# Turning norm factors straight from their column: four layers of attention and experts on one core

## The reference, cut to what matters

```python
xn = _layernorm(x)                      # (x - mean) / sqrt(var + 1e-5), over the 128 features
x = x + _L0_attn_ref(xn, ...) + _L0_ffn_ref(xn, ...)   # window attention; small mixer + 8 experts, top 2
xn = _layernorm(x)
x = x + _L1_attn_ref(xn, ...) + _L1_ffn_ref(xn, ...)   # differential attention; 8 experts, top 2
xn = _layernorm(x)
x = x + _L2_attn_ref(xn, ...) + _L2_ffn_ref(xn, ...)   # full attention; gated low-rank layer
xn = _layernorm(x)
x = x + _L3_attn_ref(xn, ...) + _L3_ffn_ref(xn, ...)   # flow attention; dequantized feed-forward
```

```python
q = rmsnorm((x @ wq.T).reshape(B, T, 16, 64), q_norm_w)
k = rmsnorm((x @ wk.T).reshape(B, T, 4, 64), k_norm_w)
```

## Time and profile before

| what | value |
|---|---|
| runs, us | 1449.86, 1451.62, 1457.27; median 1451.62 |
| profiled execution, us | 1449.79, its span 1448.0 |
| PE busy | 1291.5 us (89%) |
| DVE, ACT, POOL busy | 913.3, 664.0, 302.3 us |
| mean granted TensorE clock | 0.926 of full |

### The profile page before, as it was taken

One profiled execution on the slowest core, in us unless ns is written; L12 is line 12 of the kernel. 1 busy time (PEld: TensorE's weight loads), 2 busy tenths in 40 slices (PEclk: granted clock), 3 DMA queues, 4 the chain that ended last, 5 costly groups with the idle time before them and its releaser, 6 DMA issues.

```text
span 1448.0 us, 23894 instructions
## 1 busy us (share of the span) xinstructions
PE 1291.5 (89%) x9334; PEld 791.3 (55%) x9334; DVE 913.3 (63%) x1975; ACT 664.0 (46%) x1424; POOL 302.3 (21%) x309
## 2 busy tenths in 40 slices
PE   6878697997997888779899979999799989899998
PEld 4456565876674666445666757755344323224555
DVE  4478753343354568865687657677578868775366
ACT  2345042762651322016443535566466646576621
POOL 1242072000102510474001201044421312101000
PEclk8988698998998879759999989999999989999999
DMA  8000023332100220123523463321330121200000
GB/s 247 21 1 1 1 85 120 89 106 70 29 8 18 57 39 4 62 66 71 144 85 99 123 163 105 121 69 30 66 74 4 33 39 34 36 1 29 1 8 22
DMA packets 65101, 86.23 MB, mean 60 GB/s; under 512 B 9566, under 2 KB 49374, under 8 KB 63326
## 3 DMA queue, kind: packets, MB, share of 16 engines
q1 hardware_dynamic: 60892, 76.30, 20.1%
q0 software_dynamic: 4096, 8.40, 2.0%
HBM read 62.19 MB, written 22.48 MB: 58 GB/s over the span
## 4 chain that ended last, share of the span: by engine, by line
PE 63%; DVE 13%; DMA 9%; POOL 5%; issue 4%; ACT 3%; SPq 3%; DVEq 0%; ACTq 0%; POOLq 0%
PE psB L420 29%; PE psA L420 27%; PE psB L424 5%; DMA wA<-slots_x 3%; DVE mx L1478 2%; POOL slots_x L1945 2%; DMA arena<-scr1k 2%; PE psA L424 2%; DMA arena<-scr2k 2%; DVE st L1177 1%; ACT pbuf L1807 1%; ACT pbuf L1725 1%; DMA arena<-slots_x 1%; SPq L2049 1%; DMA scr1k<-arena 1%
## 5 line engine op out<-in xcount | busy, mean ns | idle before, releaser
L1807 ACT ACTIVATE pbuf<-psA 128x512 f32<-128x512 f32 (+3 forms) x768 | 350.6, 489 | 249.0 <-PE psA L420 241.1
L1478 DVE TENSOR_REDUCE mx<-psA 128x1 f32<-128x512 f32 (+3 forms) x520 | 326.0, 660 | 83.5 <-PE psA L420 80.7
L420 PE MATMUL psA<-arena 64*64 64x128 f32 (+6 forms) x1504 | 187.9, 291 | 2.2 <-ACT pbuf L1807 1.4
L420 PEld LDWEIGHTS psA<-arena 64*64 64x64 f32 (+3 forms) x1504 | 111.1, 135 | 70.4 <-ACT pbuf L1807 30.6
L1725 ACT ACTIVATE pbuf<-psA,st,rq 128x128 f32<-128x128 f32 x256 | 92.7, 467 | 99.9 <-DVE st L1181 99.9
L420 PE MATMUL psA<-arena,w 96*128 96x512 bf16 (+4 forms) x320 | 112.7, 404 | 6.1 <-DMA arena<-scr2k 3.3
L420 PE MATMUL psA<-w_mdiagT,w_identb 128*128 128x128 bf16 x512 | 108.8, 222 | 0.0
L420 PE MATMUL psB<-pbuf,arena 128*5 128x512 f32 (+3 forms) x1024 | 93.4, 438 | 0.5 <-ACT pbuf L1807 0.4
L420 PE MATMUL psB<-xf,wA 128*128 128x128 f32 x624 | 93.0, 294 | 0.0
L1904 POOL TENSOR_TENSOR sm<-sm,w_ohalf 128x4 f32<-128x4 f32 x24 | 24.5, 1030 | 294.7 <-DVE sm L1048 294.7
L420 PEld LDWEIGHTS psB<-xf,wA 128*128 128x128 f32 x624 | 81.5, 203 | 7.6 <-issue 2.4
(11 more groups left out here) (318 smaller groups left out, 2325.5 us busy)
## 6 DMA issues: line engine op xcount, KB each, us to landing
wA<-in_moe SPq DMA_DIRECT2D x39, 576.0 KB, 3.8
wA<-in_moe SPq DMA_DIRECT2D x39, 256.0 KB, 3.1
slots_x<-wA SPq DMA_DIRECT2D x20, 256.0 KB, 3.7
slots_y<-tH SPq DMA_DIRECT2D x18, 256.0 KB, 3.7
wA<-slots_x SPq DMA_DIRECT2D x15, 256.0 KB, 4.0
arena<-scr2k SPq DMA_DIRECT2D x48, 64.0 KB
scr1q<-arena SPq DMA_DIRECT2D x4, 384.0 KB, 3.9
scr1k<-arena SPq DMA_DIRECT2D x4, 384.0 KB, 4.2
```

The costliest lines, as they stand in the source:

```text
L420: return pe.matmul(out, lhsT, rhs, start=start, stop=stop, skip_group_check=True)
L1478: dv.tensor_reduce(m[:, t, h:h + c], maxb(lay, b, n)("mx", lay, b, n)[:, 0:c * k].rearrange("p (c k) -> p c k", c=c), AX.X, ALU.max) \
L1807: ac.activation(pb(lay, b, s, j)[:, 0:T - q0_], scoreb("ex", lay, b, s, j)[:, 0:T - q0_], ACT.Exp, bias=0.0, scale=1.0) \
```

## The change

The widened copies are gone. TensorE reads each factor column itself, with step zero along the free dimension, as the stationary operand of the transpose. It waits for GpSimd's power instead of for the copy, and gives the column tile back. VectorE's ln3 and kn0 keep only the multiply. The signals `ln_wide` and `kn_wide` go. `MERGE` is another string, with the same number of steps from each stream: 873 of the 2519 steps stand more than 10 places from where they were, most of these in layer 1 (the largest shift is 304 places).

```diff
 MERGE = (
-    "13al3cl2clclcl2clc2lclcl2c2l2cl4cl3clcl2clc2lclcl2clb3cj2cj2cbjcjc2jb4c4j3cjcbc2jc2jcb2c2jcj2cb2c2j2"
...
+    "12ala3cl2clc2l4c2lcl2c3l2cl2cl5clcl4clclc2lclc2lcb3c2j2cbjcjc2jb2c2jcj6cbc3jc2j3cbj2c2jcj2cj2cjcj4cj"
...
             def ln3(tag, b):
                 u = "ln3", tag, b
                 for w in misc.free(*u):
                     pe.wait_ge(*w)
-                pe.wait_ge(*ln_wide.at(tag, b))
-                v, bank = tA("wide", tag, b).rearrange("p (t r) -> p t r", t=4), misc(*u)
-                tr4(bank, lambda t: v[:, t, :]).then_inc(*ln_turned.up(tag, b))
-                tA.give(("wide", tag, b), ln_turned.now())
+                pe.wait_ge(*ln_pow.at(tag, b))
+                st, bank = small("ln", tag, b), misc(*u)
+                tr4(bank, lambda t: st[:, 4 + t:5 + t].to_broadcast([P, P])).then_inc(*ln_turned.up(tag, b))
+                small.give(("ln", tag, b), ln_turned.now())
...
-                pe.wait_ge(*kn_wide.at(b, kv))
-                v = tQ(*u).rearrange("p (t r) -> p t r", t=4)
-                tr4(nr(b)(*u), lambda t: v[:, t, :]).then_inc(*kn_turned.up(b, kv))
-                tQ.give(u, kn_turned.now())
+                pe.wait_ge(*ks_pow.at(b))
+                st = smq("ks", b)
+                tr4(nr(b)(*u), lambda t: st[:, 16 + 4 * kv + t:17 + 4 * kv + t].to_broadcast([P, P])).then_inc(*kn_turned.up(b, kv))
+                if kv == 3:
+                    smq.give(("ks", b), kn_turned.now())
...
             def ln3(tag, b):
-                st, dst, bank = small("ln", tag, b), ln_dst(tag, b), misc("ln3", tag, b)
-                for w in tA.free("wide", tag, b):
-                    dv.wait_ge(*w)
-                dv.wait_ge(*ln_pow.at(tag, b))
-                dv.tensor_copy(tA("wide", tag, b).rearrange("p (t r) -> p t r", t=4),
-                               st[:, 4:8].unsqueeze(2).to_broadcast([P, 4, P])).then_inc(*ln_wide.up(tag, b))
-                small.give(("ln", tag, b), ln_wide.now())
+                dst, bank = ln_dst(tag, b), misc("ln3", tag, b)
                 dv.wait_ge(*ln_turned.at(tag, b))
...
             def kn0(b, kv):
-                st, bank = smq("ks", b), nr(b)("kn", b, kv)
-                for w in tQ.free("kn", b, kv):
-                    dv.wait_ge(*w)
-                dv.wait_ge(*ks_pow.at(b))
-                dv.tensor_copy(tQ("kn", b, kv).rearrange("p (t r) -> p t r", t=4),
-                               st[:, 16 + 4 * kv:20 + 4 * kv].unsqueeze(2).to_broadcast([P, 4, P])).then_inc(*kn_wide.up(b, kv))
-                if kv == 3:
-                    smq.give(("ks", b), kn_wide.now())
+                bank = nr(b)("kn", b, kv)
                 dv.wait_ge(*kn_turned.at(b, kv))
```

More of the change, by code:

```diff
@@ L27 @@
 MERGE = (
-    "13al3cl2clclcl2clc2lclcl2c2l2cl4cl3clcl2clc2lclcl2clb3cj2cj2cbjcjc2jb4c4j3cjcbc2jc2jcb2c2jcj2cb2c2j2"
[L29 to L51, removed]
+    "12ala3cl2clc2l4c2lcl2c3l2cl2cl5clcl4clclc2lclc2lcb3c2j2cbjcjc2jb2c2jcj6cbc3jc2j3cbj2c2jcj2cj2cjcj4cj"
+    "6cbjcjcljlcbl2j2cjcj2lj3cl3j2lj5lbljcj2lj2ljl3cjcl6cjc4l3cj7cbj2cjcjbcj6cl2jb3j3cbjc2j6cl2jb2jcj2c3j"
@@ new lines @@
+    "7cbjl2j3cb2j2c2j2cj2cjcb3j3c2jcj6c3lj5l3c2jlcljl2cjcl2clcj4lcjbcjcbl2cjlj2clclbj2c3jb3c3jl2jb3jl2jb2"
+    "jl2j2l2jclalj2lbja3ja2jb2jl3jl2jljljljlj2ljlcj3dba2djbajdj2djba2jb5jb3je3jcejej2eba3j2cjbje2jec3jbaj"
+    "ejeje2ja2jejejej2ejec2j2ea3ea3ea2ec2e4c3eceded2ec3ec3ed2ec42ec2ecece2c3d2cd2cd2bc2bcd2bdbcbk2bc2bk2b"
+    "k2bc2bcbdk2bd2bkbk2bk2bdk2b2ec2bcbebecbkcebce2bk2e2bk2bkbd2b2ebcbcke2bebkebecebek2bkbebece2bke2bebe2"
+    "bke2bebe2cekbebekb2ebc2bckcdcbebecebkbebcbebebkbeke2becebkb2ebke2bebecbkbebe2bebke2bebekebebekebekec"
@@ new lines @@
+    "2b2ebcbekbec2b2ecebeke2be2bebebk2ebebebdcek2e2cbebeke2bekecebeb2cek2e2be2beckedec2kcd2ek2ce2ckd2bcdb"
+    "ebec2bk2bcbebkce2b2c2bke2b2cbce2bkecbebckbk2bcbcbc2bk2bdbkcbc2b2cbecke2beke2bkb2ebcbcebcbkbebcebcbk2"
+    "cbckbebkb2ebc2bkeb2cbec2bcbck2b2ebkbebc2bckc2e2bk2e2bkbcebekebebce2bcbece2bckebcebckece2bekcbeceb3c2"
+    "e2bk2bkb2e2ce2bece2ce2bke2beke2bekbcebcb2e2cb3ckdececebcbe2beckebecke2bcb2ec2bcebe2cekcec2bek2b2eke2"
+    "becec2bed2c2ekb2e3cecb2cebebebebck2eckceckekc2e2ckec2ekbe2bebec2bke2bcbecebc2bk2bkcbe2cb2ebkbcbk2c2b"
@@ new lines @@
+    "cbk2bcbc2bebck2beke2b2ce2bdcebkcb2cbcbek2bke2c2bek2bcbcbckb2cebck2c2e2beb2e2bekb2ebkeb2ebe2bekebe2be"
+    "bkebebkebebeke2b2ebk5bcebekeabebk2e6bkbceaekb2ek2e2b3e2bekebe2be2bebekebebekebebke2bebk2bkcbe2beae2b"
+    "ek2bebebk4b2cekakd2bck4bk4bk2dkakd4bk2bk2bkbk4bcbk4bk2bkbdbabk5beke2bkbebe2beke2bekb2e2bkbebekbebe2b"
+    "e2bekbebkb2ebdbebke2bekbe2bebebkbebebkbe2bebebkebebaekbebkbebedbebkbebdebkbe2b2ebkebebkebkbe2bebebke"
+    "be2bebke2bekbebeabebebekbebek2b2e2bkb2e2bke3bk2e2bkebebkbebec2e2bkbebebke2bebek2ek2bkd2be2bek2bkeke2"
@@ new lines @@
+    "bekebebebebaebebke2bekebebkbedebkb2e2bedbebekbeb2e2bekebeck2e2bd2bk2e2bkbebeb2ebdbek2e2bcebebke2beb2"
+    "e2bek2ebkbebebkb2ebae2bekec2b2edbebc2kea2e2bke2beke2bek2b2ekebaebebkebe2bebebek2b2ekebedebek2bkebebd"
+    "b2ebke2becbebeke2beb2e2beke2bekdb2ebkbeb2e2bekebeba2ebke2beb2e2bek2e2bkb2ebk2b3ebk2b2ec2b2e2bek2ek2e"
+    "kcek2bek2b2e2bkebebab2ebke2beabebekbebe2b2ebk2e2bkebebke2b2ebke2b2e2b2e2bek2e2baeke2bekebebkebebe2b2"
+    "e2bek2b2ekebe2b2e2bekeb2e2beabekbk2bk2babc2bdb3kck2bcfk2bgfbcbck2bg2bk2bfbg2bkbfbgbkc2bafbkbg2bk2bfb"
@@ L54 @@
+    "abk2bfbkbg2bk2bgkbf2bkbcbfbg2bkbg2bkbf2bk2bfk2bgbkbfbca2bk2bgbcbgb2kfkhfkcgk2hcagchfhachghacfi2cghi2"
+    "cih2chicicicihchi2cichcihcih3cih5ci2ci2cici3c")
 class Semaphore:
@@ L328, in build @@
         ln_mean, ln_var, ln_turned = signals("norm_tensor", 3)
-        ln_xc, ln_eps, ln_wide, ln_done = signals("norm_vector", 4)
+        ln_xc, ln_eps, ln_done = signals("norm_vector", 3)
         ln_sq = signals("norm_scalar", 1)
@@ L336, in build @@
         q_mm, ss_mm, k_mm, ks_mm, e_turned, v_mm, kn_turned = signals("project0_tensor", 7)
-        q_sb, k_c1, ss_e, ks_e, e_copied, rq_done, kn_wide, k_done = signals("project0_vector", 8)
+        q_sb, k_c1, ss_e, ks_e, e_copied, rq_done, k_done = signals("project0_vector", 7)
         q_sq, k_sq, k_c2, v_sb = signals("project0_scalar", 4)
```

## The result

The changed kernel takes 1427.8 us (median of 4, 1426.3 to 1429.6) against 1450.8 before: ratio 0.983, interval 0.980 to 0.986. A second comparison of the same two kernels gave 1425.8 against 1451.7, 0.982 (0.977 to 0.987). Forecast were 1431 us and a range of 1414 to 1447. So the number was right. The experiments show that the account under it was right in part only, and that the sum came out by luck: two errors nearly cancel.

A forecast was written before the change was run, and what follows sets the result against it. PE was taken as the bound, idle 156.5 us, 37.6 of it in waits on the two copies. Terms summed to 25.3 us, less 5 for the order: 20 off 1449.8, forecast 1431 us, range 1414 to 1447.

The forecast's parts named there:

- n0's last multiply: Four norms together at the kernel's start: last multiply ends at about 21.7 instead of 25.54, 3.9 us less.
- 4.4 of small waits: All other waits on the two copies, at h1, batch 2's keys and later norms: half of 8.8 us, 4.4.
- batch 0's keys: Key norms of batch 0: 1.2 us for the first, 0.2 for each of three more, 1.8 us.
- h2's rounds: Four norms together at h2: rounds of 1.27 us instead of 2.87, DVE setting the pace, 5.5 us less.
- the three terms: Gains ahead of 223 us: 3.9 us at n0, 5.5 at h2, 1.8 at batch 0's key norms.
- Batch 1's 0.5: Key norms of batch 1 wait for POOL's power behind the scatter DMAs; only copy and hand-over go, 0.5 us.
- batch 3's keys: Key norms of batch 3: 4.0 of 7.1 us of PE waits gained, the rest partly lost at gathered tokens.
- the memset: At 1040.13 us a copy lasted 3.72 us beside POOL's memset; PE's wait of 2.89 us goes, 2.9 us.
- a norm of layer 1: One norm of layer 1 waits 2.32 us behind a busy DVE queue; that wait goes, 2.3 us.
- The first rival: Only the chain's share: waits off the chain are slack; gain 10 to 12, time 1439 to 1442; chance 0.18.
- The order: 873 of 2519 steps move by more than 10 places; with two new waits, 5 us deducted from the gain.
- stack of layer 1's batch 3: Its transfer moves behind expert-token transfers in SP's queue; could cost 0 to 9.94 us, left in the deduction.

The follow-up runs named there:

- e5: Step-zero reads without the new order (the old MERGE string), against the kernel before: 1439.6 us, ratio 0.991 (0.988 to 0.994).
- e1: Step-zero reads with the old MERGE string, the same kernel as e5 on another chip, against the kernel before: ratio 0.9945 (0.991 to 0.998).

## Why the prediction was right, and where it was not

*What bounds the kernel, and what goes.* Right. PE's idle time is 139.1 us (about 137 forecast), DVE is busy 897.1 (893 forecast), and no VectorE copy meets a memset. PE's busy time fell by 5.1.

*The terms ahead of 223 us.* Right in size as a whole. e5 measures them without the order, and e1 repeats its places up to there within 0.3 us. n0's last multiply ends at 20.67, 4.9 us earlier (3.9 forecast). From n0 to the end of h1 the lead grows from 4.9 to 8.3, which I had only in the 4.4 of small waits. Over batch 0's keys it grows to 8.9 (1.8 forecast, 0.6 measured: it first falls to 7.2 on the products ahead of them, of which e5 runs more at the lower clock level, and the keys then add 1.7). Over h2's rounds, from first to last multiply, it grows from 9.7 to 14.8, 5.0 us (5.5 forecast; 1.18 a round against 1.27). The first scatter starts at 168.1 instead of 182.8: 14.7 us, against 11.2 in the three terms and 4.4 of small waits. Batch 1's 0.5 shows at its first multiply (15.2).

*The clock there.* The profile after has a granted clock of 0.61 in 141 to 157, near the 0.58 of before, so h2 keeps its slow pace. In n0 the four transposes behind two projections take 0.60 us, those ahead 1.11. The Trainium skill, "TensorE: Matmul & The Clock Gate", section "Part 4: PE-mode transpose", says transposes do not count as activity for the clock; here it rose behind other products, and I took the slow price. In e5, with no product between, n0's last multiply ends 1.0 us before the forecast. The reason is in its trace: from 16 to 18 us the granted clock is still 1.00, and the first eight transposes take 0.63 and 0.60 us for four, where I had 1.12. In the kernel before the level falls at 17.3 us, in the kernel after already at 15.4, while PE is busy with the variance products. Why it falls at different times behind nearly the same work stays open.

*The terms behind 223 us* failed. They were 4.0 for batch 3's keys, 2.9 for the memset, 2.3 for a norm of layer 1 and a share of the 4.4. In e5 the keys did give their time: the lead of 15.7 us at the power became 21.0 at the end of the last multiply. Then the gathered tokens and the clock took it back, to 10.9. I had seen that wait (1.54 us, "part of the gain ends there") and sized it as a small deduction. But I had not seen that the gathers stand behind the same power, so that the wait grows by what the keys save: the lead is 16.0 at the tokens, and the 4.0 came to 0.3, before the clock took 5 more. The norm gave its 2.3 (10.9 to 13.5 at layer 1's scatter). The memset's 2.9 came (13.3 to 16.3) and is gone at the next wait: PE then waits 6.71 us for the stack's load in e5, where before no wait shows. The two loads of layer 2's stacks behind it wait 4.49 and 5.21 us (3.42 and 3.33 before) and take more. PE's waits on these loads are 6.7 us before, 16.4 in e5 and 14.9 after: they grow in either order, as the next thing that is late. In all the lead is 14.7 us at the first scatter, 13.5 at layer 1's and 9.3 at the end of that profile. The first rival, that off the chain something else is late next, gave 10 to 12 us for the whole change. It is what happened to the reads alone: 12.

*The order.* Failed in sign. I took 5 us off for it, and with the reads it adds 14. I judged it by counting steps that move. What it does is spread the keys of batch 3 among attention steps and bring their power forward, so that the gathers behind it start at 415 us instead of 437 and PE has other work until the tokens come. Up to the first gather (375.7 us in e5, 375.2 and 380.9 in the two profiles of the changed kernel) it gains nothing; at layer 1's scatter it is 23 to 25 us ahead (581.0 against 558.3 and 555.7). Some 8 us of that are work of PE that moved behind the scatter (802.2 us of it there against 794.1 in e5); 14 are left at the end. The two errors, 13 us too much for the reads and 19 too little for the order, nearly cancel. That the sum came out at 1431 is luck.

*The waits that come in.* Right as places: PE waits 6.05 us for the stack of layer 1's batch 3, for the reason given (SP's queue), in the range given (0 to 9.94). The wait on POOL between ln2 and ln3 of layer 1's first norm did not show. But the wait on the stack's load, which I had named as a sign that the order took the gain back, stood beside an order that gained: as a sign of a loss in all it was wrong.

## What to carry to other kernels

What a copy between two engines costs depends on the order around it. Here the forty copies, 20 us of VectorE and 37.6 us of waits that name them, were worth 12 us in the order made for them and 67 in one that puts other work ahead of them in VectorE's queue (1492.4 against 1425.8). A copy forbids orders in which its queue has something else to wait for. So judge such a removal together with a new order, and measure both with and without each other (four kernels, one table). When you price waits that go, walk on to the next transfer on that engine's path, since everything saved ahead of it counts only up to its arrival; and look in the issuing engine's queue for what that transfer itself stands behind.

## What the runs showed of the hardware that was not expected

- A VectorE copy of 128x512 beside GpSimd memsets lasts as long as their whole run, whether it is one instruction of 3.50 us (3.72) or eight in a row of 3.77 us together (3.99). A VectorE product of 128x256 in the middle of another memset took its usual 0.42 us.
- Behind one pause of PE of 7.4 us, where there had been several short ones with about as much idle time (9.5 us against 8.6 in the 17 us ahead of the tokens), the granted clock was lower (0.83 and 0.67 against 1.00 and 0.87) and the same work took 5 us more; in a second profile 2.3 us more.
- In n0 the granted clock fell from its higher to its lower level at 15.4 us in one profile of the changed kernel and at 17.0 in another.
- A load of weights with element step zero takes what a dense one takes, 137 ns against 142.
